# An audio tower in fp32: late scatter before the expert rounds, q and k projected once and doubled by shuffles, x by single positions

## What is computed

```python
h = tok(x)            # patches of 8, 16, 32 positions at half-patch stride, each times W_i (128 x 128 p), + b + pos + scale:
                      # 127 + 63 + 31 = 221 rows of 128 per batch
h = h + attn(layernorm(h))   # q, k, v = z @ w_qkv, 8 heads of 16; softmax(q k / 4) v; @ w_agg + b_agg
x_flat = layernorm(h).reshape(-1, 128)[first 1024 rows]   # expert lists cover 1024 tokens, 2 experts of 8 each
out = out.at[token_ids].add(w * (gelu(xg @ w1[e]) @ w2[e]))   # 512 hidden units per expert
h = h + out
```

## Time and profile before

| | |
|---|---|
| median of three runs | 272.86 us |
| profiled execution | 275.58 us, span 274.1 us |
| TensorE busy | 260.4 us (95%) |
| VectorE / ScalarE / GpSimd busy | 208.2 / 142.6 / 119.8 us |
| mean granted TensorE clock | 0.986 |
| one round (c = 8 to 13) | 14.0 us |
| last step (from its first scores) | 253.7 to 274.1 |

### The profile page before, as it was taken

The page is one execution under the profiler, slowest core; times in us unless marked ns, Lnnn a source line. Parts: engine busy times, 40 slices in busy tenths (PEclk is TensorE's granted clock), DMA queues, the critical chain, the costliest instruction groups (busy, mean ns, idle before and its releaser), DMA issues.

```text
span 274.1 us, 7238 instructions
## 1 busy us (share of the span) xinstructions
PE 260.4 (95%) x2897; PEld 222.7 (81%) x2897; DVE 208.2 (76%) x450; ACT 142.6 (52%) x221; POOL 119.8 (44%) x182
## 2 busy tenths in 40 slices
PE   8999989999899999999978999999999999999982
PEld 8899978879797979797958878788888888887751
DVE  1498489979899878888853968787777777877664
ACT  3780333725252525161543768585858686859330
POOL 4000021203348473838571263838383847463223
PEclk9999999999999999999997999999999999999979
DMA  6999200099100000000021101111111110000244
GB/s 243 402 383 419 109 1 2 0 302 293 31 14 15 22 18 21 17 22 15 23 47 30 32 28 42 38 42 38 39 38 43 30 39 28 20 28 22 76 125 116
DMA packets 16391, 22.29 MB, mean 81 GB/s; under 512 B 2415, under 2 KB 10327, under 8 KB 16327
## 3 DMA queue, kind: packets, MB, share of 16 engines
q1 hardware_dynamic: 14215, 18.67, 21.0%
q0 software_dynamic: 1760, 2.60, 3.1%
q10 hardware_dynamic: 384, 0.57, 0.7%
HBM read 17.43 MB, written 5.95 MB: 85 GB/s over the span
## 4 chain that ended last, share of the span: by engine, by line
PE 78%; DVE 10%; DMA 5%; POOL 3%; issue 2%; ACT 1%; SPq 0%; DVEq 0%; POOLq 0%; ACTq 0%
PE s_ps L1224 13%; PE e_ps L1134 12%; PE s_ps L1134 9%; PE e_ps L1418 7%; PE m_ps L1338 7%; PE m_ps L1405 5%; PE m_ps L1209 5%; PE m_ps L1199 5%; DVE nmax L887 3%; PE e_ps L1405 3%; DMA g_sb<-y_rows 2%; PE m_ps L1368 2%; PE e_ps L1427 2%; PE m_ps L1188 1%; PE m_ps L1312 1%
## 5 line engine op out<-in xcount | busy, mean ns | idle before, releaser
L887 DVE TENSOR_REDUCE nmax<-s_ps 128x4 fp32r<-128x884 f32 (+1 forms) x60 | 61.8, 1071 | 15.4 <-PE s_ps L1224 15.3
L615 ACT ACTIVATE probs<-s_ps 128x888 f32<-128x888 f32 (+1 forms) x60 | 51.4, 909 | 24.3 <-PE s_ps L1224 24.3
L455 POOL TENSOR_TENSOR var_eps<-mv,eps_t 128x2 f32<-128x2 f32 x16 | 8.0, 499 | 70.2 <-DVE mv L846 70.2
L505 POOL DMA_INDIRECT y_rows<-y_sb,idx_u x23 | 23.1, 1006 | 27.4 <-PE s_ps L1224 24.7
L486 POOL DMA_INDIRECT z_slots<-z,slot_u x20 | 23.4, 1171 | 16.1 <-PE s_ps L1224 11.4
L1338 PE MATMUL m_ps<-probs,v_aug 128*32 128x221 f32 (+1 forms) x480 | 25.8, 353 | 0.0
L1418 PE MATMUL e_ps<-w_now,hidT 128*128 128x128 f32 x184 | 23.1, 275 | 0.0
L1418 PEld LDWEIGHTS e_ps<-w_now,hidT 128*128 128x128 f32 x184 | 22.4, 192 | 0.0
L901 DVE SCALAR_TENSOR_TENSOR q_lo<-q_lo,c_sb,m_ps 128x442 fp32r<-128x442 f32 x15 | 10.1, 675 | 16.0 <-PE m_ps L1312 16.0
L599 ACT COPY zT<-m_ps 128x221 f32<-128x221 f32 x16 | 5.5, 345 | 30.5 <-PE m_ps L1189 30.5
L1134 PE MATMUL e_ps<-x_hi,w_hi 128*128 128x252 f32 (+2 forms) x128 | 20.8, 295 | 0.1
(11 more groups left out here) (170 smaller groups left out, 607.9 us busy)
## 6 DMA issues: line engine op xcount, KB each, us to landing
w_raw<-wt SPq DMA_DIRECT2D x6, 512.0 KB, 9.7
x_raw<-x SPq DMA_DIRECT2D x6, 512.0 KB, 10.7
w_sb<-w SPq DMA_DIRECT2D x1, 2048.0 KB, 9.7
z_slots<-z SPq DMA_DIRECT2D x1, 1518.0 KB, 13.3
zs<-z_slots SPq DMA_DIRECT2D x7, 198.0 KB, 2.7
x_raw<-x SPq DMA_DIRECT2D x4, 256.0 KB, 5.0
out<-h SPq DMA_DIRECT2D x11, 64.0 KB
c_sb<-consts SPq DMA_DIRECT2D x1, 599.5 KB, 12.8
```

The lines of the kernel that those rows point to most:

```text
L505: g.indirect_dma_start(y_dram, bass.IndirectOffsetOnAxis(ap=idx_u[:, at:at + 1], axis=0), y_sb[:, n % 2, i, :], None).then_inc(y_out[n % 2 ...
L615: s.activation(probs[0:n, blk, 2 * f:2 * f + 2].rearrange("p t u n -> p t (u n)"), s_ps[0:n, 2 * f:2 * f + 2, 0:2 * NE], ACT.Exp, scale=DH ...
L887: v.tensor_reduce(nmax[0:n, blk, 2 * f:2 * f + 2, DH:DH + 2], src, AX_X, ALU.max, negate=True).then_inc(max_ready, 1)
```

## The change

- **Late scatter.** The last scatter of z rows (batch 4, tile 1) goes ahead of hb, which becomes `keep_h`. `zs_turn(0)` goes behind `s1(7,1)`.
- **x by single positions.** x lies as [4 phases, 128, 4 batches]; the first pieces are one phase each. Unit 0 uses three fp32r products instead of raw fp32, its taps in the order of FIRST_TAPS; w is cast in natural order, w parts 0 and 1 first.
- **Doubling.** For batches 8 to 15 q and k take one matmul each with unrepeated weights; VectorE doubles the rows with two stream shuffles each into q_d and k_d (SBUF), which the hi and lo operations then read. `project_q` stands ahead of `hidden(n,1)` in all rounds. `project_v` waits for q_d instead of q_low and, in rounds, stands ahead of `aggregate`. The v copy of batches 8 to 15 is ScalarE's.
- **Last batch.** The second `down` tile of the last round moves into the last step, and ScalarE scales both tiles (`last_y`); the exponentials go to a buffer of their own; banks, `last_pv` and `aggregate` are reordered; tile 1 of y is loaded, combined and stored first, and VectorE does all combining, around `last_norm`.

```diff
-PHASES, SIDE = 4, 2
+PHASES = 4
...
-RAW = 3
-
-WT_ORDER = (2, 3, 4, 5, 6, 7, 0, 1)
-X_PARTS = (tuple((0, 0, 256 * m, 256 * m + 256, ph, ph + 2) for m in range(2) for ph in (0, 2))
-           + tuple((g, sub, 256 * m, 256 * m + 256, 0, PHASES)
-                   for g, sub in ((0, 1), (1, 0), (1, 1)) for m in range(2)))
+X_PARTS = (tuple((0, 0, ph, ph + 1) for ph in range(PHASES))
...
+DOUBLED = 8
+
+TWICE = tuple([DH * u + i % DH for i in range(32)] for u in range(2))
...
-FIRSTS = (0, 1, 2, 0)
-SECOND = (1, 2, 0, 1)
+FIRSTS = (0, 2, 1, 0)
+SECOND = (2, 1, 0, 1)
...
+FIRST_TAPS = (0, 1, 4, 5, 2, 3, 6, 7)
...
-    products = (RAW,) if u == 0 else (0, 2, 1) if u == 1 else range(3)
-    return [(u, k, i, c) for i in range(len(pieces)) for k in products for c in range(PATCHES[scale])]
+    if u == 0:
+        return [(u, k, i, c) for k in range(3) for c in FIRST_TAPS for i in range(len(pieces))]
+    return [(u, k, i, c) for i in range(len(pieces)) for k in range(3) for c in range(PATCHES[scale])]
...
+        last_probs = w1_sb[:].rearrange("p e f -> p (e f)")[:, 0:2 * HALF * 2 * NE].rearrange(
+            "p (b t u n) -> p b t u n", b=2, t=HALF, u=2)
...
+        def q_src(b):
+            return q_d[:] if b >= DOUBLED else m_ps[:, 0, 0:2 * N].rearrange("p (u n) -> p u n", u=2)
+
+        def k_src(b):
+            return k_d[:] if b >= DOUBLED else m_ps[:, 1, 0:2 * N].rearrange("p (u n) -> p u n", u=2)
...
+                for t in (1, 0):
...
+            def keep_h(b):
...
+                if n == ROUNDS - 1:
+                    pool.wait_ge(y_last, i + 1)
+                elif i == 0:
...
+                if b == FFN_B - 1:
+                    second_scores(c, 1)
+                    scatter(b, 1, 1)
+                if c + 2 < BATCH:
+                    keep_h(c + 2)
...
+                if b >= DOUBLED:
+                    act.wait_ge(q_d_ready, 2 * (b - DOUBLED) + 2)
+                else:
+                    act.wait_ge(q_done, b + 1)
+                s.copy(q_hi[:, b % 2, :, 0:N], q_src(b)).then_inc(q_hi_ready, 1)
...
+            def last_y(i):
+
+                n, at = ROUNDS - 1, TILES_BEFORE[ROUNDS - 1] + i
+                act.wait_ge(y_last_done, i + 1)
+                if i == 0:
+                    act.wait_ge(y_out[n % 2], 16 * sum(ROUND_TILES[n % 2:n:2]))
+                    act.wait_ge(slot_w_ready, n + 1)
+                s.activation(y_sb[:, n % 2, i, :], e_ps[:, i * P:(i + 1) * P], ACT.Copy,
+                             scale=slot_w[:, at:at + 1]).then_inc(y_last, 1)
...
+                act.wait_ge(w1_ready, N_TILES)
                 for i, (banks, f, blk) in enumerate(zip(SECOND, (0, 0, 1, 1), (0, 1, 0, 1))):
                     n = TILE_N[blk]
+                    if i == 2:
+                        o_raw_copy(b - 1)
...
+            hi_w(0)
             hi_x(0)
             hi_x(1)
+            hi_w(1)
             hi_x(2)
             hi_x(3)
...
+                if n == ROUNDS - 1:
+                    last_y(0)
                 if 0 <= c < BATCH:
                     exps(c, 1)
-                if c == BATCH - 2:
-                    last_v_copy(c + 1)
+                if DOUBLED <= c + 1 < BATCH:
+                    late_v_copy(c + 1)
+                if n == ROUNDS - 1:
+                    last_y(1)
...
+            def q_double(b):
+                dve.wait_ge(q_done, b + 1)
+                for u in range(2):
+                    v.stream_shuffle(q_d[:, u, :], m_ps[:, 0, 0:N], TWICE[u]).then_inc(q_d_ready, 1)
+
+            def k_double(b):
+                dve.wait_ge(k_done, b + 1)
+                for u in range(2):
+                    v.stream_shuffle(k_d[:, u, :], m_ps[:, 1, 0:N], TWICE[u]).then_inc(k_d_ready, 1)
...
+            def combine(t, k):
+
+                dve.wait_ge(y_in[t], 16 * (len(SPANS[t]) + 1))
                 if k:
-                    dve.wait_ge(combined[0], 1)
-                v.tensor_tensor(h1k[:, :, 0, :], h1k[:, :, 0, :], g_sb[:, 0:FFN_B, k, :], ALU.add).then_inc(combined[0], 1)
+                    dve.wait_ge(combined[t], (1, 2)[t])
+                g = g_sb[:, FFN_B * t:FFN_B * (t + 1)]
+                if t == 0:
+                    v.tensor_tensor(h1k[:, :, 0, :], h1k[:, :, 0, :], g[:, :, k, :], ALU.add).then_inc(combined[0], 1)
+                else:
+                    for n, lo, hi in ((N1, 0, FFN_B - 1), (ffn_rows(FFN_B - 1, 1), FFN_B - 1, FFN_B)):
+                        v.tensor_tensor(h1k[0:n, lo:hi, 1, :], h1k[0:n, lo:hi, 1, :], g[0:n, lo:hi, k, :],
...
+            lo_x(0)
+            lo_x(1)
+            lo_w(0)
+            lo_w(1)
+            lo_x(2)
+            lo_x(3)
             lo_w(2)
             lo_w(3)
-
-            dve.wait_ge(tok_done, 1)
-            lo_x(0)
-            lo_x(1)
-            lo_x(2)
-            lo_x(3)
             lo_x(4)
             lo_x(5)
             lo_w(4)
             lo_w(5)
             lo_w(6)
             lo_w(7)
-            lo_w(0)
-            lo_w(1)
             prepare_comb()
             hT_evac(0)
             prepare_consts()
...
+                    combine(1, 0)
+                    combine(1, 1)
                     last_norm(c - 1)
+                    combine(0, 0)
+                    combine(0, 1)
                     last_residual(c - 1)
                     continue
+                doubled = DOUBLED <= c + 1 < BATCH
+                if doubled:
+                    q_double(c + 1)
...
+                if doubled:
+                    k_double(c + 1)
+                    if c + 2 < BATCH:
+                        ln_stats(c + 2)
+                    q_low(c + 1)
                 if c - 1 >= 0:
                     norm(c - 1)
-                if 0 <= c + 1 < BATCH:
+                if 0 <= c + 1 < BATCH and not doubled:
                     q_low(c + 1)
-                if c + 2 < BATCH:
+                if c + 2 < BATCH and not doubled:
                     ln_stats(c + 2)
...
-                if 0 < c + 1 < BATCH - 1:
+                if 0 < c + 1 < DOUBLED:
                     v_copy(c + 1)
                 if c == 1:
                     lo_x(8)
                 if c == 2:
                     lo_x(9)
-                if c == BATCH - 1:
-                    combine(0)
-                    combine(1)
                 if c - 1 >= 0:
                     residual(c - 1)
-                if n == ROUNDS - 1:
-                    y_evac(n)
                 if 0 <= c - 1 < FFN_B:
                     ffn_stats(c - 1)
...
+                if b >= DOUBLED:
+                    mm = pe.matmul(m_ps[:, 0, 0:N], wqkv_sb[:, 5, :], zT[:], start=True, stop=True)
+                else:
+                    for u in range(2):
+                        mm = pe.matmul(m_ps[:, 0, u * N:(u + 1) * N], wqkv_sb[:, u, :], zT[:], start=True, stop=True)
...
+                if b >= DOUBLED:
+                    pe.wait_ge(q_d_ready, 2 * (b - DOUBLED) + 2)
+                else:
+                    pe.wait_ge(q_ready, b + 1)
...
 
                 s1_pair(b, 0)
                 s1_pair(b, 1)
+                down(ROUNDS - 1, 1, ROUND)
                 s1_pair(b, 2)
                 pv(b - 1, range(0, 1))
                 s1_pair(b, 3)
                 place_pair(b, 0)
                 s2_pair_products(b, 0)
+                s2_pair_maxima(b, 0)
                 pv(b - 1, range(1, 2))
-                s2_pair_maxima(b, 0)
...
+                last_pv(b, 0)
                 aggregate(b - 1)
-                last_pv(b, 0)
...
-                if n == 0:
-                    zs_turn(0)
                 if here:
                     s1(c, 1)
                 if n == 0:
+                    zs_turn(0)
+                if ahead1:
                     project_q(c + 1)
+                if n == 0:
                     hidden(n, 0)
                 hidden(n, 1)
                 hidden(n, 2)
-                if ahead1 and n != 0:
-                    project_q(c + 1)
                 hidden(n, 3)
                 if ahead2:
...
-                ahead_of = 1 if n == ROUNDS - 1 else 2
-                down(n, 0, ahead_of)
+                down(n, 0, 1 if n == ROUNDS - 1 else 2)
                 if here:
                     s2(c, 1)
-                if behind:
+                if behind and n < 0:
                     aggregate(c - 1)
                 if ahead1:
                     project_v(c + 1)
-                down(n, ahead_of, ROUND)
+                if behind and n >= 0:
+                    aggregate(c - 1)
+                if n < ROUNDS - 1:
+                    down(n, 2, ROUND)
                 tok_some(p4)
 
...
+    once = qkv[:, 0:2].reshape(P, 2, 2, HALF, DH).transpose(0, 1, 3, 2, 4).reshape(P, 2, P)
```

145 lines of the change are left out of this document (62 added, 83 removed).

## The result

The changed kernel takes 277.07 us (median of four, 276.40 to 278.75) against 273.23 for the kernel before beside it: 1.013 of it, interval 1.0086 to 1.0173. Run again unchanged beside the third group of experiments (expected: 1.012 to 1.016, 276 to 277 us) it took 278.01 us, 1.0169 of the kernel before (1.0139 to 1.0198), a little more than expected. It is slower; the forecast was 270.7 us with a range of 267.6 to 274.2.

What follows compares the result with a forecast made beforehand. TensorE was taken as the bound, busy 13.97 of 14.00 us a round. Head +0.3, passage -3.2, rounds -0.2 and +1.0, end -0.1 sum to -2.2 us, giving 270.7 us from the 272.86 median, range 267.6 to 274.2.

Steps and rivals of the forecast that it cites:

- head +0.3: Start of the kernel: unit 0, waiting for casts, ends at 13.1 plus 0.1 for waits instead of 12.9, +0.3 us.
- passage -3.2: Last tokeniser step to first round: earlier scatter and full clock bring the transposes of h at 147.0 instead of 150.18.
- rounds -0.2 + 1.0: Expert rounds: -0.2 us for step c = 7, +0.16 in each of steps 8 to 13, together +1.0.
- end -0.1: Last steps: reordered combines and moved `down` tile nearly cancel, -0.1 us, bounds -1.2 and +1.2.
- the rival on VectorE: Rounds: VectorE becomes the bound at o_T ahead of `aggregate`, +2.8 us, 273.5, deciding from a shuffle pair of 1.1; chance 0.17.
- The step on q: Rounds: q's moved matmuls no longer fill the 0.78 us gelu wait, so the transposes of h come 0.37 us later.
- one matmul less makes the way from H to the scores 0.37 shorter: Rounds, k's projection: dropping one of its two matmuls shortens TensorE's way to the scores by 0.37 us.
- H: The transposes of the next h on TensorE (line 1180), one per round, at 192.21 and 206.21 in the profiled round.
- S - 0.64: Rounds: `aggregate`'s wait for o_T, S being the k shuffle pair's time, taken as 0.80 us: 0.16 a round.
- the step under "Sum": Total: profiled 275.58 us lay 2.7 over the 272.86 median; terms of -2.2 us applied to both, 273.4 and 270.7.
- Its upper bound: Head: at most +2.5 us, if the clock falls in the thin stretch behind the warm-up.
- the addition for VectorE: End: residual 263.9, tile 1's combine to 266.3, norm to 268.5, tile 0's combine to 270.2, residuals to 270.7, now 270.9.

Runs made afterwards that it cites:

- a1b: Changed kernel with q's projection between the second and third `hidden` tiles in rounds 1 to 6: 275.56 us, 1.0120 of the kernel before.
- a1: Changed kernel with q's projection back behind the last `hidden` tile in rounds 1 to 7: 274.43 us, 1.0049 of the kernel before.
- e1: c1 with VectorE's copy of the next round's zsT moved ahead of the turn of o: 269.77 us, 0.9871 of the kernel before.
- a3: Changed kernel with 15 instead of 10 zero matmuls ahead of unit 0 and four behind its first product: 276.30 us, 1.0118 of the kernel before.
- a5: Changed kernel with its whole end undone (combines, loads, stores, `down` tile, scaling, order of last scores): 274.51 us, 1.0043 of the kernel before.
- d1_double_alone: Kernel before with only the doubling of q and k, including q's new place: 275.02 us, 1.0107 of the kernel before.
- b1_scatter: Kernel before with only the late scatter and `zs_turn(0)` behind `s1(7,1)`: 271.62 us, 0.9942 of the kernel before.
- b2_layout: Kernel before with only x by single positions, unit 0 still on raw data: 273.16 us, 1.0018 of the kernel before.
- c1: Kernel before with late scatter, x by single positions and doubling, q's projection at its old place, old head and end: 270.33 us, 0.9926 of it.
- a4: Changed kernel with only the combines, loads and stores of y as before: 275.82 us, 1.0116 of the kernel before.
- e2: c1 with the change's combines, loads and stores of y, all combining on VectorE: 272.07 us, 0.9946 of the kernel before.

## Why the prediction was wrong

**Range and sign.** The forecast was 270.7 us and faster; the kernel is slower by 1.3 to 1.7%, above the top of the range by 2.9 us. Terms, predicted and found (second profiles): head +0.3, +0.9; tokeniser 0, -0.4; passage -3.2, -1.4; rounds -0.2 + 1.0, +2.8; end -0.1, +1.2. The signs that the prediction had named for its rivals did not point to one: rounds of 14.47 us lie above its 14.0 to 14.3 and below the 14.5 of the rival on VectorE.

**Rounds: right in half of its mechanism, wrong in its sum.** Forecast were 0.16 us a round, measured 0.47 (14.47 against 14.00). The step on q holds: a wait of 0.78 us for the gelu ahead of every turn of h, 0.38 us of it new (a1b against a1; said: 0.37), clock 1.00. What failed is "VectorE waits, TensorE follows" as an account of the other operations. I asked for the moved q only what follows it, not what it waits for: moved 1.8 us ahead, it meets ScalarE's o_raw copy (0.19 us a round, a1b). And "one matmul less makes the way from H to the scores 0.37 shorter" took k's way as TensorE's own. The chain of before showed no wait there because k's second matmul covered the zsT copy: without it `down` waits. From H to the first scores the way shrank by 0.10 us only, so VectorE cost 0.27 a round and not 0.16, and at another place: `aggregate` did not wait in the changed kernel, as the prediction's own S - 0.64 gives for the measured S; its wait appeared only when zsT's was taken away (0.25 us, e1). The rival "VectorE becomes the bound at o_T" was right in that VectorE's order held TensorE up, and wrong in the place and in its condition, S of 1.1 and more: the pair of shuffles goes from 193.62 to 194.23,

```profile
193.62 0.01 DVE L893 LOAD_MASK_SELECT k_d<-m_ps  x1
193.62 0.41 DVE L893 STREAM_SHUFFLE k_d<-m_ps 128x221 f32<-128x221 f32 x1
...
194.23 0.48 DVE L874 BATCH_NORM_STATS2 stats<-h_sb 128x6 f32<-128x128 f32 x2
...
194.91 0.59 DVE L897 TENSOR_TENSOR q_lo<-q_d,q_hi 128x442 fp32r<-128x442 f32 x1
```

so S is 0.61 and not 0.80; the mask costs 0.01 us. The Trainium skill, "VectorE: DVE Perf Modes", section "The perf-mode tier table", from which I had worked out 0.52, is nearer than the 0.80 that I took from the transposes; but one shuffle takes more than the estimate of 0.26 from its rate, 0.31 us from start to start and 0.41 by its own record. The other page I had weighed, "SBUF — State Buffer" of the Trainium skill, section "Who interferes with whom", would have q_low and k_low slower from SBUF wherever they meet a GpSimd operation that reads SBUF. They take 0.59 and 0.67 us against 0.58 and 0.67 from PSUM; only q_low had such an operation beside it (L472, 195.08 to 195.55), k_low none. So nothing of it shows there, and for k_low nothing was tested.

**Passage: right mechanism, gain read off a disturbed stretch.** The passage took 17.50 us instead of 20.47, at full clock: 2.97 less, near the 3.2. But 1.4 us of that were the clock fall of the earlier trace rows, which two of four profiles with the old order lack, and by the times (1.4 us) the median as well. The step that failed is the one under "Sum": I took the 2.7 us by which the profiled execution lay over the median as spread evenly and applied the full difference to the median, where the mean clock of 0.986 beside half clock at 145 said that a term of my sum was part of it.

**Head: the sum near, the bound used.** Its upper bound (+2.5, the clock falls in the thin stretch) is what happened in part: unit 0 ended at 14.40 us, with 0.50 at 8 to 10 us, and at 13.2 to 13.3 where the clock held (a1, a1b, a3; said: 13.2). The first H was 0.9 us later than before, and within the scatter of the old head without the fall. The tokeniser's 0.1 to 0.5 us from the layout I had set at nothing.

**End: the failed step is the addition for VectorE, and a store priced at nothing.** The addition put the residual of batch 14 at 263.9 us, because TensorE's last products were taken to come earlier. From the same start of the last step they came later, behind the moved `down` tile. The residual came at 266.52 in the first profile, with the clock at 0.50, and at 265.25 in the second, at full clock. The rest of the line followed at the predicted distances: the combine of tile 1 took 1.86 us (said: 1.8), the collision's 1.0 us did come back (0.28 us for the second product instead of 1.25), the norm ended at 269.6 in the second profile instead of the predicted 268.5, and tile 0's combine took 1.7. What was not in the sum is the way behind the last residual: with tile 0's 320 KB stored so late it takes 4.3 us, in before 3.2 and 3.1 (first and second profile); the prediction allowed 0.1. Undone, the end is 3.2 us shorter, of which 1.9 are hidden in the comparison with before, since the doubling shortens the old end (38.2 in a5 against 40.2).

## What stays open

Why the rows of y come earlier in every kernel with the doubling: the pair of loads at line 404 keeps SyncE's queue 2.64 us in the second profile of before, and the same pair (line 417) 0.92 in d1_double_alone:

```profile
257.53 2.64 SPq L404 DMA_DIRECT2D g_sb<-y_rows  x2
...
263.32 0.82 DVE L989 TENSOR_TENSOR h1k<-h1k,g_sb 128x640 f32<-128x640 f32 x1 [2.32 <-DMA g_sb<-y_rows]
...
259.54 0.92 SPq L417 DMA_DIRECT2D g_sb<-y_rows  x2
```

so before's tile 0 combine waits 2.3 us for its rows and holds the residual behind it. The first of these loads starts as long after the last turn of h in both (23.8 and 24.0 us). b1_scatter and b2_layout behave as before (end 40.1 and 40.0), c1, d1, e1 and a5 do not. Which part of the doubling does it (buffers' places, the order of GpSimd's work) was not tried. How the 3.2 us of the end split between the combines and the moved `down` tile is only bounded: 2 to 2.5 us for the combines by a4 and e2, the rest for the tile and the new order. What decides whether the clock falls behind a gap is open too: in the passage, gaps of 1.52 and 1.54 us brought it, 1.57 and 1.58 did not.

## What to carry to other kernels

An operation that is moved ahead needs two questions: what now waits behind its successor, and what it itself now finds not ready. Work that is taken off the busiest engine is a gain only up to the next operand; where the chain shows no wait, look how late each operand comes, because the removed work may be all that hid it. A clock fall in a profiled stretch is a reason for a second profile before its time is put into a sum.

## What the runs showed of the hardware

The granted clock fell to 0.50 behind gaps of 1.09 and 0.68 us in the head, and to 0.62 where the longest gap was 0.86 us; with the same longest gap it stayed at 1.00 in another profile. In the passage it fell in two profiles of four, behind 1.52 and 1.54 us of idling and not behind 1.57 and 1.58. A wait of 0.78 us in each of six rounds never lowered it, in two profiles. A stream shuffle of 128x221 out of PSUM shows 0.41 us and lets the next start after 0.31; its mask load shows 0.01. Reading x by single positions, not in pairs, made fp32r matmuls of 248 columns 5% faster (3.98 against 4.18 us for 32).
